# Spreading a block mask over 128 partitions: three DMA hops through DRAM against sixteen small matmuls and a copy, with the start loads reordered

## The reference

```
block_mask = mask.reshape(nb, 32, kb, 32).sum(axis=(1, 3)) > 0
elem_mask  = repeat(repeat(block_mask, 32, axis=0), 32, axis=1)
x = layernorm(x + einsum('bsk,nk->bsn', x, weight * elem_mask))
w = (unpack4(weight_packed) - zero_point) * scale
x = layernorm(x + einsum('bsi,oi->bso', x, w) + bias)
```

## Time and profile before

| | |
|---|---|
| median of three runs | 1480.45 us |
| profiled execution | 1485.99 us, span 1484.4 us on core 7 (1.6 us lie around it) |
| spans of the cores | 1460.5 to 1484.4 us |
| TensorE matmuls busy | 1026.3 us (69%) |
| VectorE busy | 748.8 us (50%) |
| ScalarE, GpSimd busy | 249.6 us, 132.2 us |
| stage 1 | first L340 matmul at 140.73 us, last one starts at 767.04 and runs 13.99 us |
| moved by DMA | 127.73 MB, of it 75.52 MB on the software queue |

### The profile page before, as it was taken

How to read it: one execution, slowest core, us unless ns; L and a number is a source line. 1 busy time by engine, 2 the same in 40 slices (tenths; PEclk the granted TensorE clock), 3 DMA queues, 4 the chain that set the end, 5 groups by cost and what they waited for, 6 DMA issues and landing times.

```text
span 1484.4 us, 11993 instructions; the slowest of 8 cores (1460.5 to 1484.4 us)
## 1 busy us (share of the span) xinstructions
PE 1026.3 (69%) x4468; PEld 423.9 (29%) x4468; DVE 748.8 (50%) x500; ACT 249.6 (17%) x207; POOL 132.2 (9%) x106
## 2 busy tenths in 40 slices
PE   0002669394885949699993468999999999999100
PEld 0000224141332414244440013444444444443000
DVE  0037758373763847577424994333333333333586
ACT  0000000000000000000002003434343434343100
POOL 2000000000000000000004700000000000000353
PEclk9999979697896969799995598999999999999555
DMA  9993938677483857764401001221212121210244
GB/s 140 168 169 56 135 44 112 92 115 115 56 135 42 133 96 115 115 102 73 60 0 57 1 0 41 74 85 58 85 58 83 60 82 61 80 63 29 99 193 161
DMA packets 91720, 127.73 MB, mean 86 GB/s; under 512 B 71184, under 2 KB 71184, under 8 KB 79376
## 3 DMA queue, kind: packets, MB, share of 16 engines
q0 software_dynamic: 13664, 75.52, 31.6%
q10 hardware_dynamic: 9216, 50.34, 9.3%
q1 hardware_dynamic: 68784, 1.11, 2.7%
HBM read 185.65 MB, written 17.33 MB: 137 GB/s over the span
## 4 chain that ended last, share of the span: by engine, by line
PE 46%; DMA 22%; DVE 20%; another core or an unknown queue 5%; issue 5%; ACT 1%; DVEq 0%; POOLq 0%; POOL 0%; SPq 0%; ACTq 0%
PE ps L488 29%; PE ps L340 13%; DMA em<-bmx_scr 8%; DMA bmx_scr<-bm_scr 6%; DVE crbf L234 6%; DMA bm_scr<-bmtr 5%; DVE scr_bf L287 3%; DVE arena_b L549 3%; DVE em L540 3%; DVE scr_bf L617 2%; DVE em L611 2%; DMA outT<-scr_bf 1%; PE ps L310 1%; PE ps L318 1%
## 5 line engine op out<-in xcount | busy, mean ns | idle before, releaser
L340 PE MATMUL ps<-arena_a,scr_bf 128*128 128x512 bf16 x2048 | 463.6, 388 | 139.7 <-DVE scr_bf L287 139.4
L488 PE MATMUL ps<-arena_b,scr_bf 128*128 128x512 bf16 x2048 | 461.2, 384 | 55.7 <-DVE arena_b L549 52.8
L340 PEld LDWEIGHTS ps<-arena_a,scr_bf 128*128 128x128 bf16 x2048 | 201.9, 100 | 396.3 <-issue 169.6
L488 PEld LDWEIGHTS ps<-arena_b,scr_bf 128*128 128x128 bf16 x2048 | 196.3, 98 | 319.3 <-issue 93.7
L234 DVE TENSOR_REDUCE crbf<-scr_i 128x128 bf16<-128x4096 bf16 x32 | 226.3, 7114 | 77.5 <-DMA scr_i<-maskn 77.5
L287 DVE TENSOR_TENSOR scr_bf<-scr_bf,em 128x2048 bf16<-128x2048 bf16 x64 | 143.3, 2276 | 151.7 <-DMA em<-bmx_scr 151.7
L362 ACT ACTIVATE sqst<-arena_b 128x1024 bf16<-128x1024 bf16 x32 | 33.8, 1057 | 587.4 <-DVE arena_b L355 372.3
L465 DVE TENSOR_SCALAR scr_i<-scr_i 128x2048 int32<-128x2048 int32 x32 | 39.5, 1235 | 167.1 <-DMA scr_i<-ptpr 167.1
L513 DVE TENSOR_TENSOR arena_a<-em,arena_b 128x512 bf16<-128x512 f32 x64 | 44.3, 692 | 132.8 <-ACT em L507 132.8
L355 DVE TENSOR_TENSOR arena_b<-ps,arena_a 128x512 bf16<-128x512 f32 x64 | 42.1, 673 | 129.5 <-PE ps L340 129.3
L245 PE MATMUL ps<-crbf,g8a_s 128*8 128x128 bf16 x16 | 3.6, 225 | 129.2 <-DVE crbf L234 126.5
(11 more groups left out here) (48 smaller groups left out, 305.3 us busy)
## 6 DMA issues: line engine op xcount, KB each, us to landing
scr_bf<-wtpr POOLq DMA_DIRECT2D x32, 1024.0 KB, 12.5
scr_i<-maskn POOLq DMA_DIRECT2D x32, 1024.0 KB, 22.0
scr_i<-ptpr ACTq DMA_DIRECT2D x32, 1024.0 KB, 4.8
outT<-scr_bf ACTq DMA_DIRECT2D x32, 512.0 KB, 2.7
arena_a<-xT POOLq DMA_DIRECT2D x4, 2048.0 KB, 52.0
bmx_scr<-bm_scr SPq DMA_DIRECT2D x16, 32.0 KB, 7.9
em<-bmx_scr SPq DMA_DIRECT2D x16, 32.0 KB, 4.2
bm_scr<-bmtr SPq DMA_DIRECT2D x16, 2.0 KB, 6.0
```

Source lines behind the costliest of these rows:

```text
L340: sp=(ci == C - 1): o.matmul(ps[b_][:, 0:SHW], scr_bf[:, D * (v_ % 4) + 128 * c_: D * (v_ % 4) + 128 * (c_ + 1)], arena_a[:, SC * c_ + SHW ...
L488: lambda o, w_=w, h_=h, c_=c, b_=bk, wo=woff: o.matmul(ps[b_][:, 0:SHW], scr_bf[:, wo: wo + 128], arena_b[:, SC * c_ + SHW * h_: SC * c_ + ...
```

## The change

Four edits. The constant `sel` (32 x 512, bf16) is loaded at the start: four 32 x 128 selection matrices, of which number q has a one where the row is 8q + column/16. In `mask_stage_b` the three chained DMAs are gone; in their place stand 16 matmuls of a selection matrix (stationary) by 8 columns of `bmtr`, which write the 128 x 128 pattern of the slice into PSUM bank 7, and one ScalarE copy of it into `em`. In the prologue `mask_stage_a(0)`, `mask_stage_b(0)`, `wt_mult(0)` and `mask_stage_a(1)` move ahead of most of the x loads. And `sqst` becomes another name for `mb_b`, with the tracker told of it (the mean's copy waits for readers of the square, the square for readers of the mean).

```diff
-        sqst = E(nc.sbuf_tensor("sqst", [128, SC], BF16))
+        sqst = mb_b
...
-            in_ap = bass.AP(bmtr, 0, [[KBT, rcnt], [32, jcnt], [1, 8]])
-            out_ap = bass.AP(t_bmd, 8 * m, [[KBN, rcnt], [32 * KBN, jcnt], [1, 8]])
-            dma("sync", "Q_b", out_ap, in_ap, reads=[("bmtr",)],
-                writes=[("bmd", m)], selfwait=True)
-            inr = bass.AP(t_bmd, 8 * m, [[KBN, KBN], [0, 16], [1, 8]])
-            outr = bass.AP(t_bmx, 8 * m, [[16 * KBN, KBN], [KBN, 16], [1, 8]])
-            dma("sync", "Q_b", outr, inr, reads=[("bmd", m)],
-                writes=[("bmx", m)], selfwait=True)
-            in2 = bass.AP(t_bmx, 8 * m, [[KBN, 128], [128 * KBN, C // 2], [1, 8]])
-            out2 = bass.AP(em, 8 * m, [[EMC, 128], [KBN, C // 2], [1, 8]])
-            dma("sync", "Q_b", out2, in2, reads=[("bmx", m)],
-                writes=[("EM", m)], selfwait=True)
+            for t in range(C // 2):
+                jj, qq = t // 4, t % 4
+                P("tensor",
+                  lambda o, t_=t, j_=jj, q_=qq: o.matmul(
+                      ps[7][:, 8 * t_: 8 * (t_ + 1)],
+                      sel_s[0:32, 128 * q_: 128 * (q_ + 1)],
+                      bmtr[0:32, 32 * j_: 32 * j_ + 8],
+                      start=True, stop=True, skip_group_check=True),
+                  reads=[("bmtr",), ("sel",)],
+                  writes=([("PB", 7)] if t == 0 else []), sem="S_taux",
+                  inc=(1 if t == C // 2 - 1 else 0),
+                  future=sch.plan("S_taux") if t == 0 else None)
+            emo = bass.AP(em, 8 * m, [[EMC, 128], [KBN, C // 2], [1, 8]])
+            P("scalar",
+              lambda o, a=emo: o.copy(a, ps[7][:, 0: 8 * (C // 2)]),
+              reads=[("PB", 7)], writes=[("EM", m)])
...
         wt_refill(0)
+        mask_stage_a(0)
         xq_load(0)
         if C > 1:
             wt_refill(1)
+        mask_stage_b(0)
+        wt_mult(0)
+        if NSL > 1:
+            mask_stage_a(1)
         if C > 2:
             wt_refill(2)
         for g_ in range(1, NXD):
             xq_load(g_)
-        mask_stage_a(0)
-        mask_stage_b(0)
-        wt_mult(0)
-        if NSL > 1:
-            mask_stage_a(1)
         if NSL > 2:
             mask_stage_a(2)
```

More of the change, by code:

```diff
@@ L120, in build_program @@
     t_g8b = nc.dram_tensor("g8b", [128, 8], BF16, kind="ExternalInput")
+    t_sel = nc.dram_tensor("sel", [32, 512], BF16, kind="ExternalInput")
     t_out = nc.dram_tensor("outT", [D, SC], F32, kind="ExternalOutput")
@@ L143, in build_program @@
         g8b = E(nc.sbuf_tensor("g8b_s", [128, 8], BF16))
+        sel_s = E(nc.sbuf_tensor("sel_s", [32, 512], BF16))
         zp2n = E(nc.sbuf_tensor("zp2n", [128, C], BF16))
@@ L195, in bank_ffn @@
             return FFNB[(NH * w + h) % 4]
-        smtot = ("Q_sm", 3 * 16)
+        smtot = ("Q_sm", 4 * 16)
         sgtot = ("Q_sg", 2 * 16)
@@ L203, in build_program @@
         dma("sync", "Q_sm", g8b[:], t_g8b.ap(), writes=[("g8b",)], record=smtot)
+        dma("sync", "Q_sm", sel_s[:], t_sel.ap(), writes=[("sel",)], record=smtot)
         P("vector", lambda o: o.memset(onesc[:], 1.0), writes=[("ones",)])
@@ L255, in mask_stage_b @@
               reads=[("bmb",)], writes=[("bmtr",)])
-            rcnt = min(32, KBN)
-            jcnt = (KBN + 31) // 32
-            in_ap = bass.AP(bmtr, 0, [[KBT, rcnt], [32, jcnt], [1, 8]])
-            out_ap = bass.AP(t_bmd, 8 * m, [[KBN, rcnt], [32 * KBN, jcnt], [1, 8]])
-            dma("sync", "Q_b", out_ap, in_ap, reads=[("bmtr",)],
-                writes=[("bmd", m)], selfwait=True)
-            inr = bass.AP(t_bmd, 8 * m, [[KBN, KBN], [0, 16], [1, 8]])
-            outr = bass.AP(t_bmx, 8 * m, [[16 * KBN, KBN], [KBN, 16], [1, 8]])
-            dma("sync", "Q_b", outr, inr, reads=[("bmd", m)],
-                writes=[("bmx", m)], selfwait=True)
-            in2 = bass.AP(t_bmx, 8 * m, [[KBN, 128], [128 * KBN, C // 2], [1, 8]])
-            out2 = bass.AP(em, 8 * m, [[EMC, 128], [KBN, C // 2], [1, 8]])
-            dma("sync", "Q_b", out2, in2, reads=[("bmx", m)],
-                writes=[("EM", m)], selfwait=True)
+            for t in range(C // 2):
[14 more added lines that the diff above has]
+              reads=[("PB", 7)], writes=[("EM", m)])
         def wt_refill(v):
@@ L393, in ln_finalize @@
                   reads=[("PB", pb)],
-                  writes=[(mrb_tag + "_m",), ("rows_m", seg)])
+                  writes=[(mrb_tag + "_m",), ("rows_m", seg), ("sq", 0)])
             for h in range(NH):
@@ L523, in epilogue @@
                                            AF.Square),
-              reads=[("x2", w, 0), ("x2", w, NH - 1)], writes=[("sq", 0)])
+              reads=[("x2", w, 0), ("x2", w, NH - 1)],
+              writes=[("sq", 0), ("mrb_m",)])
         q_dma(0)
@@ L671, in host_prepare @@
     g8b = (ar[:, None] // 32 + 4 == np.arange(8)[None, :]).astype(BFNP)
+    r32 = np.arange(32)
+    sel = np.concatenate(
+        [(r32[:, None] == 8 * q + ar[None, :] // 16) for q in range(4)],
+        axis=1).astype(BFNP)
     kbn = D // 32
@@ L675, in host_prepare @@
         .transpose(0, 2, 1).reshape(D, D))
-    shared = dict(wtpr=wtpr.astype(np.float32, copy=False), maskn=maskn,
+    shared = dict(wtpr=wtpr.astype(np.float32, copy=False), maskn=maskn, sel=sel,
                   ptpr=ptpr.astype(np.int32, copy=False),
```

## The result

The changed kernel takes 1599.0 us (median of 10 runs) against 1481.5 us for the kernel before (10 runs). In some runs the cores of one die show a lower clock and take longer; without these runs the ratio is 1.0785, with a 95% interval of 1.076 to 1.0809: 7.9% slower. The prediction said 9.7% slower, 1624 us with a range from 1598 to 1665. It started from 1480.45 us, and 1.0785 times that is 1596.7 us, just under its lower end. The profiled execution took 1597.17 us, with a span of 1595.5 us on core 4, against 1623.6 us that the prediction gave for a profiled execution.

A forecast was written before the change was run, and what follows sets the result against it. Stage 1 was taken as bound by the latency of three mask DMAs. X at 147.3, plus 13 x 53.1 = 690.3, plus 7.6, plus 776.8 gave span 1622.0; with 1.6 around it 1623.6 us (1624), range 1598 to 1665.

The forecast's parts named there:

- X: Time at which TensorE starts the two small block-row sums at an odd v; predicted 147.3 us for v = 1.
- Rival A: Stage 1: the odd v's product runs while the 16 selection matmuls wait; 33.7 us a slice, 1367 us total; chance 5%.
- rival B: Stage 1: clock stays low for the odd v's whole group, 27.5 us instead of 15.79; 1776 us total; chance 5%.
- rival C: Stage 1: TensorE waits, but the two mask reductions begin earlier than X; slice 46.0 us, total 1532; chance 2%.
- S: Time of the 16 selection matmuls ahead of an odd v's product: 2.5 us, bounds 1.3 to 6.9, fifteen times on the path.
- the clock: Range term for TensorE's low clock after idling, in the odd v's group: -23 to +14 us over 13 slices.
- the start: Range term for when the first product starts, after the initial loads: some 5 us either way.
- A slice: Two v of stage 1, from X to X: 19.2 + 2.5 + 16.6 + 14.8 = 53.1 us, 13 times, where it cost 42.3.
- the stand: TensorE's wait from X for VectorE's transpose, behind two mask reductions: 19.2 us in each of 13 slices.
- the odd v's group: 64 product matmuls at an odd v, starting at low clock: 16.6 us to the next group's start, bounds 14.8 to 17.7.
- v = 27: Odd v with no reduction ahead: 5.1 us plus S, 7.6 in place of 0.6; then 776.8 us to the end, unchanged.
- The prologue: Reordered loads and mask work at the start: first product at 131.4 us instead of 140.73, 9.3 us gained.

## Why the prediction was right in kind and wrong in size

**The mechanism held.** The transpose was predicted to release TensorE at X + 19.2, and it does so at X + 18.9 in twelve slices and at X + 19.8 in the first; the cause of this stand was confirmed from both sides, by moving what waits (1325.9 us) and by moving what is waited for (1479.1 us). Rival A (the product passes the waiting matmuls) is refuted by the 18.36 us of wait at 318.30, rival B (a clock low for the whole group) by groups of 16.1 us, not 27.5, rival C by reductions that start at X.

**The step that failed is S, the price of the 16 selection matmuls.** It was set at 2.5 us, with 1.3 as its lower bound, and is 0.50. I took the duration of one weight load for the spacing of two. In the changed kernel one such load lasts 99 ns, and they follow each other every 31 ns:

```profile
L262 PEld LDWEIGHTS ps<-bmtr,sel_s 32*128 32x128 bf16 x256 | 8.1, 99 | 308.7 <-issue 308.7
```

Fifteen of them on the path are 15 x 2.0 = 30 us, and the forecast of the profiled time was 26.4 us too long (1623.6 against 1597.2). The bound failed in the same way: 16 times the smallest duration isn't a lower bound for work that overlaps. The number from the Trainium skill (TensorE: Matmul & The Clock Gate, Back-to-back issue gap), 81 ns a pair, is one for 128 moving columns, and the prediction used it for 8; it too was longer than the 27 to 31 ns measured here, which decide.

**The range was drawn too narrow below.** The prediction's own bounds were -18 us for S, -23 for the clock and -5 for the start. Added up they reach 1578 us; the lower end was put at 1598 without a reason. That the measured time came out as close to it as it did is luck: the real S lies below the lower bound for S.

**The other terms.** A slice came out at 51.3 against 53.1: S -2.0, the stand -0.3 (a reduction takes 6.94 us here, 7.09 before), the odd v's group +0.4 (17.0 to the next start against 16.6). The first product came at 128.56 against 131.4, of which S is 2.0. The time from X to the product at v = 27 was 5.65 against 7.6, S again. From v = 27 to the end it is 778.4 us against 776.8. These sum to the miss: -3.1 at the first X, -23.0 for 13 slices, -2.0 and +1.6 are -26.5, and the span is 1595.5 where 1622.0 was forecast.

**The prologue** was given 9.3 us of gain; in the changed kernel it is 10 us, by experiment. The loads came as it said: the two reductions that it put at 109.5 start at 109.05. What the prediction didn't ask is what the new order is worth alone: nothing.

**What was not weighed** is that the two latencies exclude each other. The sum gave the slices 10.8 us of loss without saying that the hops' removal contributes 0 to it once the stand is there.

## What to carry to other kernels

When a DMA hop is replaced by instructions on a busy engine, ask where in that engine's list they stand and what the first of them waits for: work in the shadow of a product moves in front of it if the product is queued behind the wait. The cure is to emit the new instructions at the point where their input is sure to be ready; here the same instructions, one and a half products later in TensorE's list, turned +7.9% into -10.1%. And price short pipelined instructions by the distance of their starts: where they overlap, a duration in the trace is no bound from below.

## What was not expected of the hardware

- Matmuls with 128 weight columns and 8 moving columns follow each other every 27 to 31 ns (48 in 1.30 us, 16 in 0.50), with a granted clock of 0.50, with 32 rows as with 128, though each weight load is shown with 99 to 104 ns. A clock of 1.00 didn't shorten them: in the run with 86 filler matmuls the 16 take 0.54 us, where they take 0.56 in the changed kernel.
- A wait of 1.3 us (2.2 in the first slice) and the 16 short matmuls after it, behind 17 us of full work, were followed in 81 of 104 slices by a slower next group, and in 23 not. In the one shown, the clock was 0.73 and 0.64 in stretches of 2.4 and 3.0 us in which TensorE was busy. With the wait closed and the 16 still there, none of the 104 was slow, and the group shown took 13.97 us.
- With the old hops and the new order of loads, the two hops of 32 KB took from 46.70 to 128.35 beside the bulk loads, which another issuer's queue (GpSimd's) had under way; 53.0 and 28.3 us from issue to landing. In the run with stand and hops together, slice 1's hops fall into a quieter stretch: the three are issued at 167.52, 169.01 and 173.39, and from 160 to 260 us the two of 32 KB take 4.3 and 2.8 us.
